# An eleventh table by one-hot products in a recommendation tower, with its ids in batches

## What is computed

```python
T = jnp.concatenate([dense[:, None, :], embs], axis=1)      # (2048, 27, 128)
Z = jnp.einsum('bnd,bmd->bnm', T, T)
z = Z[:, iu0, iu1]                                           # the 351 pairs n < m
h = jnp.concatenate([z, r_dense], axis=1)                    # 479
h = jnp.maximum(h @ W_top1 + b_top1, 0.0)                    # 512
h = jnp.maximum(h @ W_top2 + b_top2, 0.0)                    # 256
y = h @ W_top3
```

## Time and profile before

| | |
|---|---|
| median of 3 runs | 458.27 us (458.07 to 464.23) |
| profiled execution | 461.09 us, its span 459.3 us |
| TensorE products | 389.6 us busy, 85% of the span |
| GpSimd | 247.2 us, 54% |
| VectorE | 231.9 us, 50% |
| ScalarE | 172.1 us, 37% |
| gathers | 256 of 0.95 us, one every 1.25 us when nothing holds them |
| TensorE's mean granted clock | 0.937 |

### The profile page before, as it was taken

One profiled execution on the slowest core, in us unless ns is written; L12 is line 12 of the kernel. 1 busy time (PEld: TensorE's weight loads), 2 busy tenths in 40 slices (PEclk: granted clock), 3 DMA queues, 4 the chain that ended last, 5 costly groups with the idle time before them and its releaser, 6 DMA issues.

```text
span 459.3 us, 9683 instructions
## 1 busy us (share of the span) xinstructions
PE 389.6 (85%) x4055; PEld 353.1 (77%) x4055; DVE 231.9 (50%) x534; ACT 172.1 (37%) x221; POOL 247.2 (54%) x263
## 2 busy tenths in 40 slices
PE   8787498879979797888979889797979889796997
PEld 6577398868878696878968778686968789694897
DVE  4478375846335544546437474456444555441131
ACT  5257435422443245151442425332451514233221
POOL 6666656555656565455655556555654556556000
PEclk9999979989989999799979999899998989799799
DMA  8972312244114412153122511144111511142230
GB/s 220 262 212 71 112 31 74 67 121 148 44 47 106 136 42 53 30 126 116 40 52 62 161 51 51 36 112 130 48 47 34 141 40 40 47 105 80 38 51 16
DMA packets 45876, 39.06 MB, mean 85 GB/s; under 512 B 32930, under 2 KB 39113, under 8 KB 45834
## 3 DMA queue, kind: packets, MB, share of 16 engines
q1 hardware_dynamic: 36014, 21.40, 17.4%
q0 software_dynamic: 8192, 16.79, 14.2%
q10 hardware_dynamic: 1628, 0.25, 0.4%
HBM read 32.40 MB, written 6.02 MB: 84 GB/s over the span
## 4 chain that ended last, share of the span: by engine, by line
PE 73%; issue 12%; ACT 7%; another core or an unknown queue 4%; DVE 3%; DVEq 0%; ACTq 0%
PE look_ps L839 31%; PE gram_ps L871 18%; PE mlp_ps L891 9%; PE look_ps L849 5%; PE mlp_ps L901 5%; ACT T L692 4%; DVE hot L521 2%; ACT T L684 1%; DVE tab_lo L498 1%; PE look_ps L943 1%; PE look_ps L830 1%; PE look_ps L913 1%; PE look_ps L935 1%; ACT T L680 1%
## 5 line engine op out<-in xcount | busy, mean ns | idle before, releaser
L481 POOL DMA_INDIRECT rows<-in_tbl_dram,ids_all x240 | 230.1, 959 | 169.5 <-issue 54.0
L839 PE MATMUL look_ps<-hot,tab_hi 125*128 125x256 f32 x616 | 165.5, 305 | 6.4 <-issue 2.9
L839 PE MATMUL look_ps<-hot,tab_lo 125*128 125x256 f32 x616 | 160.0, 296 | 0.0
L839 PEld LDWEIGHTS look_ps<-hot,tab_hi 125*128 125x128 f32 x616 | 127.0, 206 | 10.1 <-issue 5.0
L871 PE MATMUL gram_ps<-T 128*54 128x54 f32 x2048 | 85.3, 228 | 55.8 <-issue 44.6
L839 PEld LDWEIGHTS look_ps<-hot,tab_lo 125*128 125x128 f32 x616 | 127.0, 206 | 0.0
L871 PEld LDWEIGHTS gram_ps<-T 128*54 128x54 f32 x2048 | 71.4, 141 | 71.8 <-issue 55.2
L517 DVE TENSOR_TENSOR hot<-ids_near,gram_ps 125x2048 fp32r<-125x2048 f16 x40 | 90.3, 2285 | 64.9 <-PE look_ps L839 54.7
L684 ACT COPY T<-look_ps 128x512 f32<-128x512 f32 x32 | 38.3, 1196 | 169.3 <-PE look_ps L839 86.3
L692 ACT COPY T<-look_ps 128x384 f32<-128x384 f32 (+1 forms) x80 | 79.2, 1090 | 44.9 <-PE look_ps L849 38.6
L521 DVE TENSOR_SCALAR hot<-ids_near 125x256 fp32r<-125x256 f16 x320 | 73.9, 303 | 34.5 <-remote 15.2
(11 more groups left out here) (78 smaller groups left out, 164.8 us busy)
## 6 DMA issues: line engine op xcount, KB each, us to landing
dots<-gram SPq DMA_DIRECT2D x28, 182.2 KB
ids_near<-ids_rows SPq DMA_DIRECT2D x7, 640.0 KB
rows<-in_tbl_dram,ids_all POOLq DMA_INDIRECT x240
T<-in_tbl_dram SPq DMA_DIRECT2D x4, 448.0 KB
pairs<-dots SPq DMA_DIRECT2D x14, 117.0 KB
gram<-in_tbl_dram SPq DMA_DIRECT2D x3, 448.0 KB
rows<-in_r_dense_dram SPq DMA_DIRECT2D x16, 64.0 KB
pairs<-dots SPq DMA_DIRECT2D x7, 104.0 KB
```

The costliest lines, as they stand in the source:

```text
L481: pool.indirect_dma_start(rows[:, t % 2, place[n], :], None, tables[n - 1], bass.IndirectOffsetOnAxis(ap=index[:, n - 1:n].bitcast(U32), a ...
L839: mm = pe.matmul(dst, w[:VP, k, c], hot[:VP, slot, c], start=(c == 0 and half == 0), stop=(c == CH - 1 and half == 1))
```

## The change

From unit 2 on (`ADDED`) an eleventh table, number 16 of the 26 (vector 17), is looked up by products, as the last of a unit; in units 0 and 1 it is gathered as before. Its raw rows are loaded to the place of `w2` after the others, and `w2` is loaded once they have been split (`LATE`). From unit 2 on the fourth round has two vectors in place of three, and the look groups are (0,1), (2,3), (4,5), (6,7), (8,9), (10). The tables that unit 0 takes whole are 7, 8 and 9, and the order of the first loads and splits follows.

The ids of a unit come in batches of three rows (192 KB), to a ring of nine places; a batch is ordered once the batch three before it has been compared. ScalarE no longer converts them: VectorE compares the ids with `numbers`, which holds 8 times the partition plus 0 to 7, as a broadcast operand (copied to PSUM, `steps`) or as a per-partition scalar. In unit 1 six compares and in unit 2 all but two are broadcast ones now. GpSimd's pace has its own table (`STEP_LESS`) for 15 gathers a tile. The wait before blocks 1 and 3 now stands in unit 1 too.

```diff
-ONEHOT = 10
+ONEHOT = 11
...
     onehot = sorted(small[-7:] + small[:first])
     runs = []
     for n in range(nt + 1):
@@ -33,7 +33,10 @@
             runs[-1].append(n)
         else:
             runs.append([n])
-    return onehot, runs[1:] + runs[:1]
+    rounds = runs[1:] + runs[:1]
+
+    added = [f for f in small if f not in onehot and any(r[0] == f + 1 and len(r) > 1 for r in rounds)][-1]
+    return onehot + [added], rounds, [[n for n in r if n != added + 1] for r in rounds]
...
-    LOOKS_FIRST = ((1, 0), (3, 2), (5, 4), (6, 7), (8,), (9,))
-    LOOKS = ((0, 2), (4, 6), (7, 8), (9, 1), (3,), (5,))
-    WHOLE = (1, 3, 5)
...
+    LOOKS_FIRST = ((7, 0), (8, 1), (9, 2), (3, 4), (5,), (6,))
+    LOOKS_SECOND = ((0, 1), (2, 3), (4, 5), (6, 7), (8,), (9,))
+    LOOKS = ((0, 1), (2, 3), (4, 5), (6, 7), (8, 9), (10,))
+    FEW = 10
+    ADDED = 2
+    WHOLE = (7, 8, 9)
+    LATE = 10
+
+    LEADING = (0, 7, 1, 8, 2, 3, 9, 4, 5, 6, 10)
+    BATCH = 3
+    BATCHES = 3
...
-        ids_near = sb("ids_near", [P, 2, K, Q], F16)
+        ids_near = sb("ids_near", [P, BATCHES * BATCH, Q], F16)
+        numbers = sb("numbers", [P, CH], F32)
...
+        raw += [table_at(w2[:].rearrange("p c f -> p (c f)"), 0)]
...
+        def rounds_of(u):
+            return rounds_more if u < ADDED else rounds_less
+
+        def rows_count(u, r):
+
+            return 16 * sum(len(rounds_of(v)[r]) - (r == dense_round) for v in range(u + 1))
...
+        def hands_before(u):
+            return FEW * u if u <= ADDED else FEW * ADDED + K * (u - ADDED)
 
         def by_steps(u, at):
 
 
-            return u >= 3 and at not in (3, 9)
+            return at in (2, 3, 4, 5, 8, 9) if u == 1 else u >= 2 and at not in (3, 9)
...
+        def ids_used(b):
+
+            if b < BATCHES:
+                return min(BATCH * (b + 1), FEW - 2)
+            u, at = (BATCH * (b - BATCHES + 1) - 1) // K + 1, (BATCH * (b - BATCHES + 1) - 1) % K
+            return min(hands_before(u) + at + 1, hands_before(u + 1))
...
-            def load_ids_near(u):
-                if u >= 2:
-                    sp.wait_ge(hot_ready, K * (u - 1))
-                sp.dma_start(ids_near[:, u % 2], ids_rows[u:u + 1].rearrange("u k q -> u (k q)")
-                             .to_broadcast([P, K * Q])).then_inc(ids_near_landed[u % 2], 16)
+            def load_ids_near(b):
+                first, end = K + BATCH * b, min(K + BATCH * (b + 1), K * UNITS)
+                place = b % BATCHES * BATCH
+                sp.wait_ge(hot_ready, ids_used(b))
+                sp.dma_start(ids_near[:, place:place + end - first], ids_rows.rearrange("u k q -> (u k q)")[first * Q:end * Q]
+                             .rearrange("(o x) -> o x", o=1).to_broadcast([P, (end - first) * Q])
+                             ).then_inc(ids_near_landed[b % BATCHES], 16)
...
+            batch, batches = 3, -(-K * END // BATCH)
             for u in range(END):
                 load_dense(u + 1, 0)
-                if u + 2 < UNITS:
-                    load_ids_near(u + 2)
+                while batch < batches and BATCH * (batch - 2) <= K * u + 2:
...
+                while batch < batches and BATCH * (batch - 2) <= K * u + 7:
...
+                while batch < batches and BATCH * (batch - 2) <= K * u + 9:
+                    load_ids_near(batch)
+                    batch += 1
                 if u == 0:
                     load_pair_weights(1)
+                    sp.wait_ge(lo_ready, lo_count(LATE))
                     sp.dma_start(w2[:], W2.rearrange("(c p) f -> p c f", p=P)).then_inc(weights_landed, 16)
...
-            STEP_OF = (4, 5, 6, 6, 8, 8, 8, 10, 10, 11, 12, 12, 13, 13, 15, 16, 16, 17, 18, 19, 20, 21, 21, 22, 23, 23, 24, 25, 26, 26, 27, 28)
+            nc.gpsimd.iota(numbers[:], pattern=[[1, CH]], base=0, channel_multiplier=CH,
+                           allow_small_or_imprecise_dtypes=True).then_inc(numbers_ready, 1)
+
+            STEP_MORE = (4, 5, 6, 6, 8, 8, 8, 10, 10, 11, 12, 12, 13, 13, 15, 16, 16, 17, 18, 19, 20, 21, 21, 22, 23, 23, 24, 25, 26, 26, 27, 28)
+            STEP_LESS = (4, 5, 6, 6, 8, 8, 8, 10, 10, 11, 12, 12, 13, 15, 16, 16, 17, 18, 19, 20, 21, 21, 22, 23, 24, 25, 26, 27, 28, 29)
...
-                late = [looked(7), looked(8), looked(9), looked(10)]
+                late = [looked(k + 1) for k in range(6, len(in_order(u + 1)))]
...
-                k = (looked if u else looked_first)[at]
+                k = in_order(u)[at]
+                count = hands_before(u) + at
                 if u == 0:
-                    dve.wait_ge(ids_relative, 1 if at == 0 else k // 2 * 2 + 2)
+                    dve.wait_ge(ids_relative, at // 2 * 2 + (2 if at else 1))
+                    near = ids_near[:VP, at] if at < FEW - 2 else ids_near_end[:VP, at - FEW + 2]
                 else:
-                    dve.wait_ge(ids_relative, K * (u + 1))
-                if K * u + at >= 2:
-                    dve.wait_ge(hot_looked, K * u + at - 1)
+                    b, place = (K * (u - 1) + at) // BATCH, (K * (u - 1) + at) % (BATCH * BATCHES)
+                    dve.wait_ge(ids_near_landed[b % BATCHES], 16 * (b // BATCHES + 1))
+                    near = ids_near[:VP, place]
...
-                        eq = nc.vector.tensor_scalar(hot[:VP, at % 2, c], ids_near[:VP, u % 2, k], float(c), None,
-                                                     ALU.is_equal)
-                        if u == 0 and at == 0 and c == CH // 2 - 1:
+                        number = numbers[:VP, c:c + 1] if u else float(c)
+                        eq = nc.vector.tensor_scalar(hot[:VP, count % 2, c], near, number, None, ALU.is_equal)
...
+            nc.vector.tensor_copy(steps, numbers[:]).then_inc(steps_ready, 1)
...
+            split(LATE)
...
+                    if u + 1 >= ADDED:
+                        compare(u + 1, 10)
...
-            def make_relative(u):
-                act.wait_ge(ids_near_landed[u % 2], 16 * ((u + 1) // 2))
-                nc.scalar.activation(ids_near[:VP, u % 2], ids_near[:VP, u % 2], ACT.Identity,
-                                     bias=minus_row[:VP]).then_inc(ids_relative, K)
...
-                if b % 2 == 1 and 1 < u < END:
-                    pe.wait_ge(hot_ready, K * (u + 1) + (2 if l == 0 else 8) + (b == 3 and (l == 0 or u + 1 < END)))
+                    pe.wait_ge(steps_ready, 1)
+                if b % 2 == 1 and 0 < u < END:
+                    pe.wait_ge(hot_ready, hands_before(u + 1) + (2 if l == 0 else 8) + (b == 3 and (l == 0 or u + 1 < END)))
```

126 lines of the change are left out of this document (70 added, 56 removed).

## The result

The changed kernel takes 448.24 us (446.97 to 449.66) against 461.25 us (458.07 to 468.55) for the kernel before on the same chip: 0.9731 of it, interval 0.9671 to 0.9792. So it is some 12 us faster, where I had forecast 3. The profiled execution took 448.83 us, with a span of 447.0 us against 459.3 us.

The account below looks back on a forecast made before the run. TensorE bounds the kernel, its dots held up by GpSimd's gathers in flight. Terms 12.1 - 1.3 + 2.4 + 0.9 - 8.75 - 3 - 4 - 1.5 = -3.2 us from 458.27 give 455.1 us; 8-in-10 range 443 to 468 us.

Parts of the forecast that it names:

- within 2%: Whole kernel: a time of 449.1 to 467.4 us, about what a measurement cannot tell from no change; chance 0.60.
- the three return terms: TensorE time expected back from fewer gathers: shorter dots -8.75 us, turn at a unit's end -3, clock -4.
- Added lookups: TensorE, six units from unit 2 on: eleventh table's products at 2.01 us each, on the path, +12.1 us.
- VectorE's new compare: Unit's second half: TensorE waits for table 10's compare, 0.4 us a unit (bounds 0 and 1), together +2.4 us.
- Gathers: Second tile's dots: burst one gather shorter, TensorE released 1.25 us earlier, seven times, -8.75 us.
- The turn at a unit's end: Before the next unit's dots: transposes' signal passes between gathers 8 and 9, -0.5 us a unit, -3 us (ends 0, -10.8).
- The clock: Lookups behind stalled dots: fewer falls to 1.2 GHz, a third taken back, -4 us (ends 0 and -12.6).
- Rival 2: Returns are whole: second tile's dots stay at 2.4 GHz, turn free in half the units, about 444 us; chance 0.22.
- rival 1: Gathers are not what breaks up the dots; only work is added, +12.6 us, 470.9 us; chance 0.15.
- rival 3: Ids come late behind SyncE's waits, more likely one at the start, about 458 us; chance 0.08.
- The ends of the terms: All terms' extremes taken together, from -30 to +18 us, called far wider than is likely.
- Per-partition scalars at nothing: VectorE's remaining compares: at most 0.6 us each, two a unit, hidden behind the table before; 0 us, upper end +3.

Follow-up runs that it names:

- e1: The changed kernel, but the eleventh table is still gathered as well from unit 2 on, its rows unused: 471.58 us, 1.0109 of the kernel before.
- e5: The kernel before, with no gathers from tile 4 on, working on old rows: 391.13 us, one execution.
- e6: The kernel before, with each gather from tile 4 on replaced by a plain load of the table's first 128 rows: 381.19 us, one execution.
- e8: The changed kernel, with compare and products of the eleventh table cut to one eighth: 445.03 us, 0.9654 of the kernel before.
- e9: The kernel before, with the products of each unit's last table done twice from unit 2 on: 467.27 us, 1.0137 of the kernel before.
- e2: The kernel before without the twelve gathers and their transposes, and without the eleventh lookup: 456.4 us, 0.969 of the kernel before.

## Why the prediction was right and wrong

The time lay in the range and on the right side, but the likeliest value was 7 us too high, and 3 us of its nearness were luck: it was reckoned from 458.27 us, and beside the changed kernel the kernel before took 461.25. As a change it was -3.2 us against some -12, and "within 2%", which I gave 0.60, did not come. The mechanism was right (e1, e5, e6); what failed is the size of the three return terms. Over the five middle units they were -6.25 for the dots, -2.5 for the turn and -3.5 for the clock, together -12.25, and measured -11.1, -6.6 and -6.4, together -24.1. Point by point:

- **Added lookups, +12.1 us.** Right as work: 4.03 us a pair at the full clock. But e8 and e9 put their net cost at a quarter to a half of their length (2.6 to 3.9 of 10.6, 6.3 of 12.1).
- **VectorE's new compare, +2.4 us.** Too low: 0.78 us a unit in place of 0.4, within the bounds that I gave (0 to 1). I had counted 0.3 us of lateness and only 0.1 for the hand-overs. In unit 6, where one of the last compares has a per-partition scalar, there are three waits, of 0.78, 0.43 and 0.27 us.
- **Gathers, -8.75 us.** The 1.25 us a unit for the second tile's burst were met (5.2 to 5.6 us became 4.0, against the rows above): 7.1 us over five units where I had 6.25. What I missed is that the other dots change too. The first tile's dots lost 0.4 to 0.5 us of gaps at their start in three units, 2.2 in one and none in one, and 0.4 to 0.8 us in their second part (3.8 to 4.2 us became 3.4). So the dots gave 11.1 us. I had costed only the dots in whose burst the gather itself had stood. In microseconds this is the largest of the three misses, 4.9.
- **The turn at a unit's end, -3 us.** This is the term that was furthest off by its factor, 2.6. The reasoning was that the signal should pass between gathers 8 and 9, and so it does. But I took -0.5 of 1.8 us, for fear that gather 11 would take it back in the next dots. It did not: the wait went (to 0.2 us everywhere) and the first dots run with no gap, or once in a profile with 0.2 to 0.35 us of one. Measured, 6.6 us over five units. e1, e2, e8 and e9 show whose doing this is: not the missing gathers', but the 2 us of the eleventh lookup, during which GpSimd runs through what is due and comes to a pause.
- **The clock, -4 us.** Mis-sized: the lookups alone got 6.4 us back. I took a third of the falls; in the profile 125 long distances between lookup products became 63, and units 4 and 5 have a granted clock of 1.00, the other three 0.97. e1, with the gathers back, has 0.94 again.
- **The three returns have one cause and rise or fall together.** I wrote this and still took two of them near their lower ends (-3 of -10.8, -4 of -12.6) and the third for one stretch of dots alone. That is the error in the sum: where the dots' stall is short and the turn is won, fewer lookups fall to the lower clock. Rival 2 (444 us, chance 0.22) described the mechanism better than the forecast did; rival 1 is refuted by e1, e5 and e6; nothing in the list of waits speaks for rival 3.
- **The ends of the terms.** I gave them as -30 to +18 us; the ends as I stated them add up to about -23 and +21. The range did not rest on this sum.
- **The start.** I had put 0.9 us for broadcast compares, -1.5 us for ScalarE, and shares of the other terms, together about -1 us up to unit 2's first dots. It is 3.2 us later in this profile; in two more profiles of the same kernel unit 2's dots begin at 156.6 and 159.9 us. But e2 and e9, which are the kernel before up to unit 2, have them at 158.7 and 156.4 us, where its own profile has 152.1. So the 3.2 us are within what one kernel's starts differ by, and neither my -1 us nor its opposite is shown. One thing seen there is ScalarE kept waiting until 54.98 us, 2.75 us after a gather that started at 52.23 in a run of gathers. No experiment cut the start apart: it stays open.
- **Per-partition scalars at nothing.** Their price is 2.33 us against 1.73 a compare, as the upper bound had it, and in the middle units it is hidden, as I said, except in unit 6.

## What to carry to other kernels

Price work added to the busiest engine by what it stands beside, not by its length: long products at a place where the engine otherwise waits for a delayed signal cost here a quarter to a half of themselves. When one cause makes several losses (gaps, late signals, a fallen clock), take their returns as one case, whole or nothing, and not each at a cautious share. Cost a removed disturbance at every stretch that it touches, not only at the one where it stood. And before tuning the spacing of a disturbance, ask whether it is removed or only moved: three settings of the pace gave nothing.
